# A feed-forward chunk cut into three steps of a common order of engine programs

## The reference

```python
x = x + tanh(g_xattn[0]) * L0_xattn(layernorm(x), ctx, ctx)      # 16 heads of 8, mask
x = x + tanh(g_ffn[0])   * L0_ffn(layernorm(x))                  # 64 small relu networks
x = x + tanh(g_xattn[1]) * L1_xattn(layernorm(x), ctx, ctx)      # a temperature for each head
x = x + tanh(g_ffn[1])   * L1_ffn(layernorm(x))                  # 4 experts, 512 wide, best 2
x = x + tanh(g_xattn[2]) * L2_xattn(layernorm(x), ctx, ctx, key_mask)
x = x + tanh(g_ffn[2])   * L2_ffn(layernorm(x))                  # 8 experts, 352 wide, best 2
x = x + tanh(g_xattn[3]) * L3_xattn(layernorm(x), ctx, mask)
x = x + tanh(g_ffn[3])   * L3_ffn(layernorm(x))                  # 8 linear experts, best 2
```

## Time and profile before

| | us |
|---|---|
| median of three runs | 1237.0 |
| lowest and highest run | 1235.21, 1238.47 |
| the profiled execution | 1225.93 |
| its span, first to last instruction | 1224.2 |
| TensorE busy | 987.4 |
| VectorE busy | 713.9 |
| ScalarE busy | 462.0 |

### The profile page before, as it was taken

How to read it: one execution, slowest core, us unless ns; L and a number is a source line. 1 busy time by engine, 2 the same in 40 slices (tenths; PEclk the granted TensorE clock), 3 DMA queues, 4 the chain that set the end, 5 groups by cost and what they waited for, 6 DMA issues and landing times.

```text
span 1224.2 us, 14483 instructions
## 1 busy us (share of the span) xinstructions
PE 987.4 (81%) x4795; PEld 659.0 (54%) x4795; DVE 713.9 (58%) x2190; ACT 462.0 (38%) x1101; POOL 105.7 (9%) x175
## 2 busy tenths in 40 slices
PE   3477988986877877876889889989989888789866
PEld 2333443443332565464566656667667666567754
DVE  1853351438183594496365665756765677666755
ACT  2334435457476354454425316315315211212210
POOL 2100000003030130021000100100100100000000
PEclk9678999988696897898889989989989988989987
DMA  9200000000000000000000000000000000000000
GB/s 270 82 1 1 1 1 0 1 1 1 1 1 1 1 1 0 1 1 1 1 1 1 1 1 1 2 0 1 1 1 1 1 1 9 1 9 1 1 9 9
DMA packets 12065, 12.72 MB, mean 10 GB/s; under 512 B 3758, under 2 KB 7896, under 8 KB 11992
## 3 DMA queue, kind: packets, MB, share of 16 engines
q10 hardware_dynamic: 5536, 8.04, 2.2%
q1 hardware_dynamic: 6072, 3.24, 1.0%
q0 software_dynamic: 384, 0.53, 0.2%
HBM read 10.75 MB, written 1.05 MB: 10 GB/s over the span
## 4 chain that ended last, share of the span: by engine, by line
PE 54%; DVE 27%; ACT 9%; issue 4%; POOL 1%; POOLq 0%; ACTq 0%; DVEq 0%
PE bank L1554 7%; PE bank L1542 5%; PE bank L1466 5%; PE bank L1544 5%; PE bank L1543 5%; DVE hb L1244 4%; PE bank L1352 4%; PE bank L1481 3%; DVE nm L1109 3%; DVE x L1262 3%; DVE hb L1248 3%; DVE x L1233 2%; ACT PTs L917 2%; ACT hb L951 2%; PE bank L1319 2%
## 5 line engine op out<-in xcount | busy, mean ns | idle before, releaser
L951 ACT ACTIVATE hb<-bank 96x512 f32<-96x512 f32 (+1 forms) x160 | 95.2, 595 | 337.7 <-PE bank L1544 337.5
L1244 DVE SCALAR_TENSOR_TENSOR hb<-hb,bank 96x512 f32<-96x512 f32 (+1 forms) x160 | 109.2, 682 | 184.1 <-ACT hb L951 183.6
L1554 PEld LDWEIGHTS bank<-m_w,hb 128*128 128x128 f32 (+1 forms) x1280 | 178.7, 203 | 23.4 <-issue 3.5
L1554 PE MATMUL bank<-m_w,hb 128*128 128x128 f32 (+1 forms) x1280 | 180.0, 286 | 0.4
L1542 PE MATMUL bank<-parts,m_w_lo 128*96 128x512 f32 (+1 forms) x320 | 155.1, 485 | 14.9 <-DVE hb L1244 14.9
L1543 PE MATMUL bank<-parts,m_w_hi 128*96 128x512 f32 (+1 forms) x320 | 137.4, 429 | 0.0
L1544 PE MATMUL bank<-parts,m_w_hi 128*96 128x512 f32 (+1 forms) x320 | 137.2, 429 | 0.0
L1248 DVE TENSOR_TENSOR hb<-hb,bank 96x512 f32<-96x512 f32 (+1 forms) x160 | 109.7, 686 | 5.5
L1364 PE MATMUL bank<-KT,Qs 96*128 96x308 f32 x192 | 78.2, 426 | 42.0 <-ACT PTs L863 21.2
L1481 PE MATMUL bank<-Qs,KT 112*77 112x512 f32 x192 | 95.6, 529 | 16.4 <-ACT PTs L917 14.3
L1542 PEld LDWEIGHTS bank<-parts,m_w_lo 128*96 128x96 f32 (+1 forms) x320 | 64.8, 203 | 52.8 <-DVE hb L1244 20.7
(11 more groups left out here) (271 smaller groups left out, 1543.5 us busy)
## 6 DMA issues: line engine op xcount, KB each, us to landing
m_w<-in_L_ffn_w_dram ACTq DMA_DIRECT2D x2, 1024.0 KB, 11.3
nat_m<-in_L_ffn_W_dram ACTq DMA_DIRECT2D x1, 1408.0 KB, 16.8
x<-in_x_dram SPq DMA_DIRECT2D x4, 256.0 KB, 7.8
out_dram<-x SPq DMA_DIRECT2D x4, 256.0 KB, 2.0
f_out<-in_L_ffn_Wout_dram POOLq DMA_DIRECT2D x8, 64.0 KB, 7.7
m_w<-in_L_ffn_W_experts_dram ACTq DMA_DIRECT2D x1, 512.0 KB, 16.8
ctxn<-in_ctx_dram SPq DMA_DIRECT2D x4, 38.5 KB
Wq<-in_L_xattn_Wq_dram SPq DMA_DIRECT2D x2, 64.0 KB
```

The costliest lines, as they stand in the source:

```text
L951: act.activation(hb[n % 3][0:m, :], bank[TURN[0]][0:m, :], ACT.Tanh, scale=0.5).then_inc(*chunk_act.up(u, n))
L1244: dve.scalar_tensor_tensor(out=h, in0=h, scalar=1.0, in1=bank[TURN[0]][0:m, :], op0=ALU.add, op1=ALU.mult) \
L1554: op = pe.matmul(bank[7][:, t * P:(t + 1) * P], hb[n % 3][0:m, t * P:(t + 1) * P], wd, start=i == 0 and t == 0, stop=ends_expert(k, n) and ...
```

## The change

The step of a chunk becomes three: up, gate, down. ScalarE's tanh stands in the second, both operations of VectorE and the addition to x in the third. For F0 a chunk is two steps: up, then down of the chunk before, with the relu in the second. The weights of the steps in the common order are new: 0.7, 0.7 and 1.1 for a chunk, 0.1, 0.1 and 1.1 for each of the last two (which hold only a down), 0.9 and 0.9 for F0. No instruction is added, removed or altered; semaphores, banks and buffers are the same.

```diff
--- before.py
+++ after.py
@@ -700,7 +700,7 @@
     def steps_body(k):
         if k in MHA:
             return H + 1
-        return {"A3": 3, "F0": C0 + 1, "F3": len(tiles)}.get(k) or len(chunks[k]) + LATE
+        return {"A3": 3, "F0": 2 * (C0 + 1), "F3": len(tiles)}.get(k) or 3 * (len(chunks[k]) + LATE)
 
     def steps_tail(k):
         return 7 if k in MHA else 2 if k == "F0" else 0
@@ -716,6 +716,13 @@
     def steps_f(u):
         return steps_body(kind(u)) + steps_tail(kind(u))
 
+    def weights_f(u):
+
+        k = kind(u)
+        if k == "F0":
+            return [0.9, 0.9] * (C0 + 1) + [1.0] * steps_tail(k)
+        return [0.7, 0.7, 1.1] * len(chunks[k]) + [0.1, 0.1, 1.1] * LATE
+
 
     beside = [[i + LAG] for i in range(ATTENTIONS - LAG)] + [[12, 13, 14, 15], [16, 17]]
 
@@ -724,7 +731,7 @@
         yield from "A" * len(weights_a(("A", 0)))
         yield from merged(weights_a(("A", 1)), [1.0] * steps_pre("F0"))
         for i in range(ATTENTIONS):
-            yield from merged([w for j in beside[i] for w in weights_a(("A", j))], [1.0] * steps_f(("F", i)))
+            yield from merged([w for j in beside[i] for w in weights_a(("A", j))], weights_f(("F", i)))
         for j in (18, 19):
             yield from "A" * len(weights_a(("A", j)))
 
@@ -938,19 +945,23 @@
 
                 if k == "F0":
                     for c in range(C0):
+                        yield
                         act.wait_ge(*chunk_psum.at(u, c))
                         room_in(c)
                         act.activation(hb[c % 3], bank[TURN[c % 2]][:], ACT.Relu, scale=f0_cols[:, 0, c:c + 1],
                                        bias=f0_cols[:, 1, c:c + 1]).then_inc(*chunk_act.up(u, c))
                         yield
                     yield
+                    yield
                 if k in chunks:
                     for n, (e, i, o, m) in enumerate(chunks[k]):
+                        yield
                         act.wait_ge(*chunk_psum.at(u, n, "up"))
                         room_in(n)
                         act.activation(hb[n % 3][0:m, :], bank[TURN[0]][0:m, :], ACT.Tanh, scale=0.5).then_inc(*chunk_act.up(u, n))
                         yield
-                    for _ in range(LATE):
+                        yield
+                    for _ in range(3 * LATE):
                         yield
                 if k == "F3":
                     for _ in tiles:
@@ -1224,7 +1235,7 @@
                     yield
                     return
                 if k == "F0":
-                    for c in range(C0 + 1):
+                    for _ in range(steps_body(k)):
                         yield
                 def gated(e):
 
@@ -1236,16 +1247,23 @@
 
                 if k in chunks:
                     todo = chunks[k]
+                    def gate(n):
+                        m = todo[n][3]
+                        h = hb[n % 3][0:m, :]
+                        dve.wait_ge(*chunk_silu.at(u, n))
+                        dve.wait_ge(*chunk_psum.at(u, n))
+                        dve.tensor_tensor(h, h, bank[TURN[1]][0:m, :], ALU.mult).then_inc(*chunk_ready.up(u, n))
+
                     for n in range(len(todo) + LATE):
+                        yield
+                        yield
                         if n < len(todo):
                             e, i, o, m = todo[n]
                             h = hb[n % 3][0:m, :]
                             dve.wait_ge(*chunk_act.at(u, n))
                             dve.scalar_tensor_tensor(out=h, in0=h, scalar=1.0, in1=bank[TURN[0]][0:m, :], op0=ALU.add, op1=ALU.mult) \
                                 .then_inc(*chunk_silu.up(u, n))
-                            dve.wait_ge(*chunk_silu.at(u, n))
-                            dve.wait_ge(*chunk_psum.at(u, n))
-                            dve.tensor_tensor(h, h, bank[TURN[1]][0:m, :], ALU.mult).then_inc(*chunk_ready.up(u, n))
+                            gate(n)
                         if n >= LATE and ends_expert(k, n - LATE):
                             gated(todo[n - LATE][0])
                         yield
```

## The result

The changed kernel took 1161.05 us (median of 4 runs, 1155.49 to 1166.6), beside 1236.11 us for the kernel before: a ratio of 0.9393, 95% interval 0.9344 to 0.9442. That is 75 us less, where 19 were forecast, and outside the range (1196 to 1250).

A forecast was written before the change was run, and what follows sets the result against it. The prediction took TensorE to lead, sharing the chain's end with other engines, with 160 us idle to win in feed-forward work. Its terms, -28.3 + 14.9 - 6 = -19.4 us, gave 1218 us from 1237, range 1196 to 1250.

The forecast's parts named there:

- the sum: TensorE's idle time in feed-forward work: 13.4 us less, from -28.3 for gaps and +14.9 for late silu.
- This idle time of VectorE is not on the path where TensorE leads, so I book no gain.: VectorE's 183.6 us of silu waiting for the tanh: expected to fall under 60 us, with no time gained.
- Hidden by gate: ScalarE's tanh (0.595 us) moved behind attention steps costs nothing, since TensorE's gate matmuls (0.70 us) cover it.
- Gaps open to a finer order (-28.3): Attention steps' waits on TensorE, 70.8 us, that later feed-forward matmuls could fill: 40% taken as gained, -28.3 us.
- the named six: The six TensorE waits called open: maxima (two), heads' exponential, normalised rows, q's low part, divided result; 70.8 us together.
- Silu comes late (+14.9): The next up on TensorE waits for VectorE's silu, now made later: the 14.9 us wait doubles, +14.9 us.
- The rival on this side: Silu comes late, 0.3 us in each chunk, costing 48 us: 1257 us, chance 0.13.
- Blocks: Block stretches of F1 with A1: VectorE is the bound, finer order can't help, and they still take 30 us.
- The weights: New step weights put downs and gates among steps dividing and turning the result; counted within the 40%, no cost.
- The clock (-6): Less TensorE idle time raises its clock from 0.90 to 0.912, worth 11 us, of which 54% taken: -6 us.
- The rival by which short bursts lower the clock: F1 beside A1 falls from clock 0.88 to 0.76, costing 24 us: 1248 us, chance 0.09.
- The fourth rival: Gaps close nearly all and silu isn't late: -50, -12 for clock, 15 back for overlap, 1192 us; chance 0.15.

The follow-up runs named there:

- run 3: Kernel after, but in F1 and F2 TensorE issues up, gate and down in the first step; tanh second, VectorE third: 1195.22 us, 0.9673 of before.
- run 6: Kernel after, but ScalarE's tanh stands in the first step, beside up: 1160.15 us, 0.9414 of before.
- run 4: Kernel after, but VectorE makes silu in the second step, with the tanh, and the product in the third: 1168.66 us, 0.9475 of before.
- run 5: Kernel after, but VectorE does both operations in the second step, with the tanh and the gate matmuls: 1182.59 us, 0.9592 of before.
- run 11: The kernel after measured again, unchanged, on the chip of runs that varied its pieces and weights: 1151.13 us, 0.9336 of before.
- run 10: Kernel after with chunk weights 0.5, 0.5 and 1.5 in place of 0.7, 0.7 and 1.1: 1167.12 us, 0.9452 of before.
- Run 8: Kernel after, but VectorE's product with the gate result is put off to the next chunk's first step: 1187.78 us, 0.9622 of before.
- run 1: Kernel after with the old weights split over the new steps (1/3 each; 0.5 for F0): 1154.77 us, 0.9388 of before.
- run 2: Kernel before, a chunk in one step, with the new weights as sums (2.5, 1.3, and 1.8 for F0): 1229.13 us, 0.9974 of before.

## Why the prediction was wrong

The direction was right, the size far off: the profiles show 59 us, of which 45 are idle time of TensorE in the stages with feed-forward work (166 to 121 us from about 157 us to the end of the last feed-forward unit, at 1178.4 and 1118.5), where the sum had 13.

**The step that failed: "This idle time of VectorE is not on the path where TensorE leads, so I book no gain."** Run 3 changes VectorE's and ScalarE's place and leaves TensorE's chunk whole: it gives 40 us (0.9673 of 1236). Run 6 shows no effect of the tanh's place in the kernel after, and runs 4 and 5 that VectorE's is worth some 10 us (17 beside run 11) and 25 us with TensorE in pieces. A wait isn't cheap because its engine has time: in the timeline above, what stood behind silu in VectorE's program was attention's work, for which TensorE then waited. The rows were at hand. L1319, L1364 and L1381 behind VectorE were 47.9 us, and I read them as gaps that matmuls could fill, not as work held up by the 183.6 us before silu; in run 3, with no matmul of F1 or F2 moved to fill them, they are 16.2. Nor did the wait for the tanh fall as far as the prediction said: it is 94.0 us, not under 60. "Hidden by gate" was wrong with it, though run 6 finds no cost in it.

**Gaps open to a finer order (-28.3).** 36.0 us went, 51% and not 40%, and L1481 and L1381 more than halved, as forecast. But the reason was only half right. Run 3 lowers the four waits for VectorE as far without any finer order on TensorE in F1 and F2, and leaves L1499 at 14.2. The pieces as such closed the heads' wait. The wait for the divided result, which the weights were to shorten, stayed (8.6 and 8.1). Beyond the named six, the small waits that I priced at nothing fell as well, by some 22 us.

**Silu comes late (+14.9).** The wait grew by 20.0 us, so the size was close; the L1562 row is 34.9 where about 30 was forecast. What it costs was not: in runs 5 and 10 this wait was 13 and 10 us shorter (beside the first profile after and run 11) and the time rose or stayed. It can't be added as a term of its own, since silu early is other work late. The rival on this side needed 45 us of this wait; run 3 has 52.3 and is still faster than before. What it misjudged was the same thing, what VectorE wins by being late. Run 8 is that rival come true for the product: a wait of 51.7 us, and 2.3% of the time lost.

**Blocks.** Right: in the first unit of F1 with A1 they take 34.8 and 34.7 us from the first L1364 to L1381, before and after (the 30 us of the prediction were a part of that). VectorE is busy 32.9 and 32.0 us of it, and so the 26 us that this stage won lie outside the blocks.

**The weights.** They entered only as part of the 40%. Runs 1 and 2 show no effect on the time.

**The clock (-6).** This term was sized too small as well. From 158 us to the end of the feed-forward work the clock rose from 0.90 to 0.92 in the profiles and TensorE's busy time fell by 16 us (the means of the whole span are both 0.891, because the first 62 us, in which TensorE is busy for a third, had 0.81 before and 0.69 after). The 16 us of the result that the profiles don't show came with a higher clock too. No run isolates why the clock is higher. The rival by which short bursts lower the clock did not come true: F1 beside A1 went from 0.88 to 0.90, with chunks in pieces a third as long. Nor did the pieces raise it, as far as can be seen: run 2, with whole chunks, has 0.90 in that stage too. The rule of the Trainium skill (TensorE: Matmul & The Clock Gate, A second HAM failure mode: psum-queue depth-cycling), that short idle spells between groups make the clock swing, shows no effect here: the traces have 0.90 for the shorter bursts, and 0.88 and 0.90 for the longer.

**Two slips in the working.** The fourth rival's sum, -50 and -12 and 15 back, is -47 and not -45. And 0.3% as what a measurement of this kernel can tell is too fine: 26 executions of the kernel before lie between 1223.44 and 1239.92 us, 1.3% apart, and the intervals of the ratios are some 0.5 to 0.8% to either side for four executions.

What stays open: how the 40 us of run 3 come about in full. Its profile shows 30 of them: TensorE's idle time is 218.9 us, 17.9 less than before, and its busy time 12.5 less, at a mean clock of 0.898 against 0.891. And the nine waits of the earlier trace rows are no shorter in sum, 118.2 us before and 117.5 in run 3: what the attention work won there, the wait for silu took, and the idle time that went lay in the smaller waits. That VectorE's new place gives the time is measured; by which of the small waits, and by how much through the clock, is not shown. Run 3 moves the tanh as well, and run 6 prices the tanh's place only with TensorE in pieces. And run 5 is only the nearest to TensorE in pieces with VectorE at its old place; the old place itself, one step earlier, was not tried.

## What to carry to other kernels

Where several engines follow one hand-written order, try each operation one step behind what it waits for: the same step as its producer and two steps behind it were both slower for VectorE here. An engine that stands before a result just being issued holds up everything behind it (here 1.75 and 2.96 us at a time), and that cost shows as another engine's wait for that other work, under another name. Before you cut steps finer, look at the longest wait of an engine with a queue behind it, and read who waits for what stands there; moving the consumers, VectorE's operations and the tanh, to later steps gave 3.3% here with the chunk's matmuls left whole, and too late a step for the product lost 2.3%.

## What the hardware did that I had not expected

The mean clock varies between executions of one and the same kernel by enough to matter. The kernel after, in its first profile and in run 11 (span, mean granted clock):

```profile
core 0: 1164.9 us, clock 0.891
```

```profile
core 0: 1146.5 us, clock 0.915
```

18.4 us lie between them, with almost the same waits (34.9 and 36.8 us for silu, 16.6 and 18.7 for A1's exponentials). So a difference of up to 1.6% between two single profiles of this kernel need not be one of the code.
